# The last tile of the last chunk: a DMA transpose replaced by eleven TensorE transposes

## The reference, cut to what matters

```python
xn = _layernorm(x)
# attention: weights = exp(tanh((xn W + b) xn^T * 1/|i-j|)), zero diagonal, rows normalised, times xn
# experts, per token, for the two chosen ones, score = sigmoid(xn gate_w^T):
h = square(relu((xn * score) @ w_up[e].T))      # 176 wide, bf16
routed = h @ w_down[e].T                        # bf16 operands
# shared expert: square(relu(xn @ shared_up.T)) @ shared_down.T
out = x + attention + sum(routed) + shared
```

## Time and profile before

| | us |
|---|---|
| median of 3 runs | 129.37 (129.23 to 129.52) |
| the profiled execution's own time | 129.49 |
| its span | 127.6 |
| TensorE matmul busy / weight load busy | 116.4 / 84.6 |
| VectorE / ScalarE / GpSimd busy | 109.9 / 82.5 / 63.8 |

### The profile page before, as it was taken

How to read it: one execution, slowest core, us unless ns; L and a number is a source line. 1 busy time by engine, 2 the same in 40 slices (tenths; PEclk the granted TensorE clock), 3 DMA queues, 4 the chain that set the end, 5 groups by cost and what they waited for, 6 DMA issues and landing times.

```text
span 127.6 us, 2805 instructions
## 1 busy us (share of the span) xinstructions
PE 116.4 (91%) x960; PEld 84.6 (66%) x960; DVE 109.9 (86%) x331; ACT 82.5 (65%) x106; POOL 63.8 (50%) x114
## 2 busy tenths in 40 slices
PE   3977787789999999999999999999999999999961
PEld 3954255457757884778567875778477856667951
DVE  5796898989999999999999999999999699968511
ACT  1226577688488927893689647983789378966400
POOL 5339719974954386437743695339643004431000
PEclk9999999999999999999999999999999999999997
DMA  3998003976666494559756866686768955698681
GB/s 86 386 406 322 12 0 43 156 145 113 113 113 116 133 177 86 99 129 115 143 97 115 189 113 113 118 181 128 99 122 133 149 107 98 155 147 169 129 213 65
DMA packets 49260, 17.65 MB, mean 138 GB/s; under 512 B 46432, under 2 KB 47200, under 8 KB 49248
## 3 DMA queue, kind: packets, MB, share of 16 engines
q1 hardware_dynamic: 48672, 15.83, 61.9%
q10 hardware_dynamic: 576, 1.66, 3.5%
HBM read 3.85 MB, written 2.10 MB: 47 GB/s over the span
## 4 chain that ended last, share of the span: by engine, by line
PE 79%; DVE 11%; DMA 3%; issue 2%; ACT 2%; POOL 1%; POOLq 0%; ACTq 0%
PE h_ps L633 14%; PE out_ps L659 12%; PE dots L587 10%; PE side L604 10%; DVE gated L467 6%; PE out_ps L651 6%; PE side L616 4%; PE small L579 4%; PE out_ps L666 4%; PE out_ps L648 4%; PE small L560 3%; DMA hiddenT<-hidden 3%; PE side L621 3%; PE small L568 2%; DVE resid L479 1%
## 5 line engine op out<-in xcount | busy, mean ns | idle before, releaser
L341 ACT ACTIVATE hidden<-gated 128x1408 bf16<-128x1408 bf16 x32 | 43.9, 1376 | 17.3 <-DVE gated L467 17.3
L467 DVE SCALAR_TENSOR_TENSOR gated<-h_ps,gates 128x1408 bf16<-128x1408 f32 x32 | 51.6, 1613 | 3.2 <-PE h_ps L633 3.2
L633 PE MATMUL h_ps<-upT,xnTb 128*128 128x512 bf16 (+1 forms) x96 | 24.3, 362 | 1.5 <-DVE gated L467 1.5
L225 POOL TENSOR_SCALAR xn<-x_sb,meanvar,rstd 128x128 f32<-128x128 f32 x28 | 22.0, 800 | 0.6
L659 PEld LDWEIGHTS out_ps<-downT,hiddenT 128*128 128x128 bf16 x308 | 19.4, 98 | 3.3
L659 PE MATMUL out_ps<-downT,hiddenT 128*128 128x128 bf16 x308 | 21.4, 219 | 0.0
L258 POOL TENSOR_TENSOR shidden<-srelu 128x512 f32<-128x512 f32 (+1 forms) x16 | 13.2, 828 | 15.4 <-ACT srelu L335 15.3
L251 POOL TENSOR_SCALAR_AFFINE_SELECT probs<-probs 128x256 f32<-128x256 f32 x16 | 6.6, 410 | 26.2 <-ACT probs L329 26.2
L587 PE MATMUL dots<-projT,xnT 128*128 128x256 f32 x60 | 16.4, 396 | 1.7 <-ACT projT L320 1.5
L604 PE MATMUL side<-xn,probs 128*128 128x129 f32 x128 | 17.0, 275 | 0.6 <-DVE resid L479 0.6
L604 PEld LDWEIGHTS side<-xn,probs 128*128 128x128 f32 x128 | 16.0, 192 | 2.1 <-issue 1.3
(11 more groups left out here) (84 smaller groups left out, 152.1 us busy)
## 6 DMA issues: line engine op xcount, KB each, us to landing
x_sb<-in_x SPq DMA_DIRECT2D x7, 256.0 KB, 9.1
out_y<-final SPq DMA_DIRECT2D x7, 256.0 KB, 2.6
up_raw<-in_up ACTq DMA_DIRECT2D x1, 704.0 KB, 7.0
down_raw<-in_down ACTq DMA_DIRECT2D x1, 704.0 KB, 9.0
hiddenT<-hidden SPq DMA_TRANSPOSE x32, 3.5
out_y<-final SPq DMA_DIRECT2D x2, 128.0 KB, 1.9
late_sb<-in_late SPq DMA_DIRECT2D x1, 224.0 KB, 7.1
x_sb<-in_x ACTq DMA_DIRECT2D x1, 128.0 KB, 2.8
```

The lines of the kernel that those rows point to most:

```text
L225: g.tensor_scalar(xn[:, c, t, 0:D], x_sb[:, c, t, :], meanvar[:, c % 2, t, 0:1], rstd[:, c % 2, t:t + 1], ALU.subtract, ALU.mult).then_inc ...
L341: a.activation(hidden[:, t, :], gated[:, t, :], ACT.Square).then_inc(squared, 1)
L467: v.scalar_tensor_tensor(out=gated[:, t, :].rearrange("p (e h) -> p e h", e=E), in0=h_ps[:, 0:NH].rearrange("p (e h) -> p e h", e=E), scal ...
L633: last = t_.matmul(h_ps[:, at:to], xnTb[:, c % 4, t * P:(t + 1) * P], upT[:, at:to], start=True, stop=True)
```

## The change

For tile 3 of the last chunk alone, `turn` is no longer called. In its place:

- `gate_last` gates the tile in two instructions of 704 columns (four experts each) where one of 1408 did it.
- `square_last` squares it in two instructions of 704 columns.
- `turn_last`, put between `down_tile(7,0)` and `down_tile(7,1)` on TensorE, turns the eleven 128 x 128 blocks with `transpose` against a bf16 identity, in parts of 4, 4 and 3 blocks, one part per bank of `h_ps`, which is free by then.
- ScalarE copies parts 0 and 2 to `hiddenT`, VectorE copies part 1, between `finish(6)` and `finish_last(0)`.
- `down_last` is `down_tile(7,3)` with a wait per part.
- GpSimd makes the bf16 identity once (`narrow_ident`), in step 0 after `cast_down`.

```diff
+        ident_b = sb("ident_b", [P, P], BF16)
+        HALF = NH // 2
+        def turn_at(part):
+            return h_ps[:, part * CH:(part + 1) * CH].bitcast(BF16)
+        PARTS = ((0, 4), (4, 8), (8, KT))
 # SyncE
-            for t in range(TILES):
+            for t in range(TILES - 1):
                 turn(LAST, t)
             store(LAST - 1)
 # GpSimd
+            def narrow_ident():
+                pool.wait_ge(ident_made, 1)
+                g.tensor_copy(ident_b[:, :], ident[:, :]).then_inc(ident_narrowed, 1)
                 if k == 0:
                     cast_down()
+                    narrow_ident()
 # ScalarE
+            def square_last():
+                par, t = LAST % 2, TILES - 1
+                act.wait_ge(hT_loaded[1 - par][t], hT_count(LAST - 1))
+                act.wait_ge(half_taken, 1)
+                a.activation(hidden[:, t, 0:HALF], gated[:, t, 0:HALF], ACT.Square).then_inc(half_squared, 1)
+                act.wait_ge(h_taken, TILES * NCH)
+                a.activation(hidden[:, t, HALF:NH], gated[:, t, HALF:NH], ACT.Square).then_inc(squared, 1)
-            square(NCH - 1, 3)
+            square_last()
+            for n, part in enumerate((0, 2)):
+                at, to = PARTS[part]
+                act.wait_ge(turned, part + 1)
+                a.activation(hiddenT[:, LAST % 2, TILES - 1, at:to, :].rearrange("p j n -> p (j n)"),
+                             turn_at(part)[:, 0:(to - at) * P], ACT.Copy).then_inc(turned_taken[part], 1)
 # VectorE
-            gate(LAST, 3)
+            gate_last()
             finish(LAST - 1)
+            at, to = PARTS[1]
+            dve.wait_ge(turned, 2)
+            dve.wait_ge(out_made, TILES * (LAST - 1))
+            v.tensor_copy(hiddenT[:, LAST % 2, TILES - 1, at:to, :].rearrange("p j n -> p (j n)"),
+                          turn_at(1)[:, 0:(to - at) * P]).then_inc(turned_taken[1], 1)
 # TensorE
+            def turn_last():
+                pe.wait_ge(ident_narrowed, 1)
+                for part, (at, to) in enumerate(PARTS):
+                    if part == 0:
+                        pe.wait_ge(half_squared, 1)
+                        pe.wait_ge(half_taken, 1)
+                    if part == 1:
+                        pe.wait_ge(squared, TILES * NCH)
+                    for j in range(at, to):
+                        last = t_.transpose(turn_at(part)[:, (j - at) * P:(j - at + 1) * P],
+                                            hidden[:, TILES - 1, j * P:(j + 1) * P], ident_b[:, :])
+                    last.then_inc(turned, 1)
+            def down_last():
+                c, t = LAST, TILES - 1
+                for part, (at, to) in enumerate(PARTS):
+                    pe.wait_ge(turned_taken[part], 1)
+                    for j in range(at, to):
+                        last = t_.matmul(out_at(c, t), hiddenT[:, c % 2, t, j, :], downT[:, j, :],
+                                         start=False, stop=(j == KT - 1), skip_group_check=True)
+                last.then_inc(out_made, 1)
-            for t in range(TILES):
-                down_tile(c, t)
+            down_tile(c, 0)
+            turn_last()
+            down_tile(c, 1)
+            down_tile(c, 2)
+            down_last()
```

More of the change, by code:

```diff
@@ L123, in moe_attention_kernel @@
         h_made, h_taken, squared = sem("h_made"), sem("h_taken"), sem("squared")
+        half_taken, half_squared = sem("half_taken"), sem("half_squared")
+        ident_narrowed, turned, turned_taken = sem("ident_narrowed"), sem("turned"), [sem(f"turned_taken{part}") for part in range(3)]
         hT_loaded = [[sem(f"hT_loaded{par}{t}") for t in range(TILES)] for par in range(2)]
@@ L128, in moe_attention_kernel @@
         WARM = 12
+        HALF = NH // 2
+        CUT = 5
         def wait(engine, s, value):
@@ L469, in gate, with gate_last @@
                                        op0=ALU.max, op1=ALU.mult).then_inc(h_taken, 1)
+            def gate_last():
+                t = TILES - 1
+                dve.wait_ge(h_made, TILES * NCH)
+                dve.wait_ge(squared, TILES * LAST)
+                for half in range(2):
+                    cols = slice(half * HALF, (half + 1) * HALF)
+                    share = gates[:, LAST % 2, t, half * E // 2:(half + 1) * E // 2].rearrange(
+                        "p (e a) -> p e a", a=1).to_broadcast([P, E // 2, HID])
+                    v.scalar_tensor_tensor(out=gated[:, t, cols].rearrange("p (e h) -> p e h", e=E // 2),
+                                           in0=h_ps[:, cols].rearrange("p (e h) -> p e h", e=E // 2), scalar=0.0,
+                                           in1=share, op0=ALU.max, op1=ALU.mult
+                                           ).then_inc(h_taken if half else half_taken, 1)
             def attend(c, q):
```

## The result

| | us | ratio to before |
|---|---|---|
| before, median of 6 runs | 129.34 (129.20 to 129.52) | |
| after, median of 6 runs | 128.44 (128.27 to 128.53) | 0.9928, 95% interval 0.9915 to 0.9941 |

The change makes the kernel 0.90 us faster (0.76 to 1.10 by the interval). Forecast were 128.6 and a gain of 0.74. The time is inside the range. The gain is a little larger than the sum; the interval begins just above the forecast, and the profile says where more can come from.

The account below looks back on a forecast made before the run. TensorE's 1.40 us idle gap before the last down tile was the prize: -1.40 + 0.61 (transposes) + 0.05 (waits) = -0.74 us, from the median 129.37 to 128.6, range 128.3 to 129.1.

Parts of the forecast that it names:

- The bound: Before the last down tile: TensorE idles 1.40 us, the most that removing tile 3's DMA transpose can give back.
- The transposes: On TensorE before down_tile(7,1): eleven bf16 transposes at 0.056 each add 0.61 us; upper bounds 1.08 and 1.42.
- the rival in which a record is a pitch: TensorE's eleven transposes: each costs the fp32 record of 0.273, 3.00 us in all, time 131.0; chance 0.03.
- The waits: In turn_last and down_last on TensorE: seven waits, already met, cost 0.05 us together, 0.2 at most.
- The halves: Tile 3's gate and square in two instructions each: gates end 0.25 us later, hidden with 1.3 to spare.
- The copies: ScalarE and VectorE copies to hiddenT: 0.59, under 0.69 and 0.48 us, hidden, last ready 0.38 before down_last.
- The moved stores: SyncE's queue: store(6) leaves about 120.25 instead of 122.14; last two stores 1.3 us apart instead of 2.6.
- No rival here: Late operand beside the early store, 128.9 to 129.1, chance 0.09; last store landing in 2.1, 129.0, tail or front 0.07.
- The signs: Expected in the profile after: last down tile from 123.5, last copy near 123.1, store(6) 120.3, last add 124.35, span 126.9.
- The identity: narrow_ident on GpSimd in step 0, under 0.30 us: costs 0, or 0.3 with the cover gone.
- Cost 0: Term for narrow_ident on GpSimd: the mask might come 0.05 us late, nothing added to the time.

Follow-up runs that it names:

- the second experiment: Kernel after with gate and square of the last tile in halves, but the whole tile turned by one DMA transpose, no TensorE transposes: 128.65 us, ratio 0.9932.
- the kernel with six blocks: Kernel after with blocks 0 to 4 turned by a DMA transpose and only blocks 5 to 10 by TensorE: 128.42 us, again 128.69; ratios 0.9927 and 0.9932.

## Why the prediction was right, step by step

**The bound.** The prize was put at 1.40 us of TensorE idle time, not at the transfer's 3.51. With the transfer gone the tail is 0.80 shorter, 1.40 less the 0.61 of the transposes. Shown.

**The transposes.** Put at 0.61 from the matmul's pitch, with 1.08 and 1.42 as bounds; measured 0.61 (121.15 to 121.76), and doubled 1.23. The record of one is 219 ns, that of a down matmul, and in the stream only a quarter of it is paid, so the rival in which a record is a pitch is refuted. The Trainium skill (TensorE: Matmul & The Clock Gate, Part 4: PE-mode transpose) has about 275 ns for one in a kernel, which is nearer to the record here than to the pitch of 56 ns; as a pitch it would have been 3.03 us for the eleven.

**The waits.** 0.05 for seven satisfied waits was too much: from `turn_last` to `down_last` TensorE's groups follow each other at 0.61 or 0.62 (121.15, 121.76, 122.37, 122.99), so together they cost about 0.01. This is why the tail gave 0.80 and not 0.74.

**The halves.** They were called a cost of 0.25, hidden behind 1.3 us. The cover was right (1.48: squares done at 119.67, wanted at 121.15). The sign was wrong: two gates take 1.69 and not 1.84, and as the first square runs beside the second gate, gate to last square is 2.51 (117.16 to 119.67) where it was 3.04 (117.65 to 120.69). The prediction's own lines had it: they end the second square at 120.32, where the whole one ended at 120.70. Hidden in after, so the sum did not suffer; alone it is the 0.51 of the second experiment.

**The copies.** ScalarE's took 597 and 485 ns (0.59 and 0.48 forecast). VectorE's took 424 ns where 0.69 was the bound; it moves 384 columns in 357 ns in the kernel with six blocks, so about 0.52 ns a column, twice as fast as the gate's 0.99, which reads fp32 from PSUM. The Trainium skill (VectorE: DVE Perf Modes, Why PSUM operands drop a tier) allows a PSUM operand a two-fold mode, and not for fp32; for this bf16 copy the trace agrees. The slack was 0.44 where 0.38 was forecast.

**The moved stores.** `store(6)` left at 119.72, beside the transfer of tile 2, which was not late. `store_last(1)` followed 1.2 us behind `store_last(0)` and landed 1.7 after its issue, as before. No rival here took place.

**The signs.** With the 0.49 that after's profile was ahead when the tail began added back, the last down tile starts at 123.48, the last copy ends at 123.04, `store(6)` goes at 120.21 and the last add starts at 124.29, all within 0.1 of what was written. One sign was badly written: a distance from the last add to the end of the span past 2.1 was to mean "wrong". It was 2.54 before the change already, and the forecast's own 124.35 and 126.9 put it at 2.55; the 2.1 is the latency of a store. The distance did not grow beyond 2.56, so what the sign was meant to catch did not happen, but as written it could not have told.

**The identity.** It was costed at 0, with 0.3 as the price if the cover were gone. It does not cost time, it moves GpSimd, and the traces credit it with 0.21. With the waits that makes 0.80 + 0.21 = 1.01 by the traces, where 0.74 was forecast; the measured 0.90 lies between, and its interval, 0.76 to 1.10, cannot tell how much of the 0.21 is in it. The mechanism of the tail was right; the term that was wrong is "Cost 0": a shift in time was treated as harmless when its consumers had slack, and the engine beside it was not looked at. That this miss was small is luck: nothing in the prediction bounded what a shift of GpSimd does to VectorE.

## What to carry to other kernels

When a tail waits for a transfer, find the first moment at which the consumer's queue is free. That gap, not the latency, is the prize, and what the replacement adds to that queue is its price. Put the new producer as far ahead in the queue as its input allows, so that the copies behind it run under other work: here that was 0.47 of 0.80 us. Where several parts of a change shorten the same path, time each alone: halving the work of the path gave 0.51 for nothing on TensorE, and adds nothing to a change that takes the path away. And compare the executions' times beside the profiles: with five blocks by DMA the span got shorter and the time did not follow.

## What the runs showed of the hardware beyond that

- A bf16 128x128 transpose in a stream of matmuls costs 0.056 us on TensorE, record 219 ns, weight load 98 ns, at a granted clock of 1.00 (the 2.4 GHz level).
- In the tail the issue of a DMA transpose of a 128x1408 bf16 tile holds SyncE 1.38 to 1.39 us and the data land 3.5 us after it (up to 5.3 over the run); with five blocks of 128 columns it holds SyncE 1.43 to 1.46 us, with six 1.24, and both land after 2.8. So about a fifth of the latency goes when the size is halved.
- VectorE's match, 128x32 fp32 from SBUF, takes 177 to 194 ns, or up to 683 ns beside a GpSimd instruction, and then ends at a fixed distance from that one's start. The chain passes through a match in step 1 alone.
